# One of a body's four weight loads issued behind the key and query writes instead of in front of them

## The reference

```python
q, k, v = layernorm(x) @ Wq + bq, ctx @ Wk + bk, ctx @ Wv + bv      # split into 16 heads
attn = softmax(where(mask, -1e15, q @ k.T / 4))
x = x + tanh(g_xattn) * ((attn @ v) @ Wo + bo)
y = layernorm(x)
w = top 3 of softmax(tanh(mean(y) @ W1 + b1) @ W2 + b2), scaled to sum 1
x = x + tanh(g_ffn) * (y + sum over e of w[e] * (gelu(y @ Wa[e]) @ Wb[e]))
```

## Time and profile before

| | us |
|---|---|
| median of 3 runs | 319.05 (318.33 to 320.27) |
| the profiled execution | 319.47 |
| span of its profile | 317.7 |
| first phase, to the first matmul of the feed-forward | about 192.4 |
| TensorE busy | 293.0 (92%) |
| granted TensorE clock, mean | 0.973 |

### The profile page before, as it was taken

How to read it: one execution, slowest core, us unless ns; L and a number is a source line. 1 busy time by engine, 2 the same in 40 slices (tenths; PEclk the granted TensorE clock), 3 DMA queues, 4 the chain that set the end, 5 groups by cost and what they waited for, 6 DMA issues and landing times.

```text
span 317.7 us, 10417 instructions
## 1 busy us (share of the span) xinstructions
PE 293.0 (92%) x3968; PEld 242.0 (76%) x3968; DVE 227.3 (72%) x648; ACT 223.8 (70%) x439; POOL 136.4 (43%) x191
## 2 busy tenths in 40 slices
PE   7876997997999999999899876999999999999996
PEld 6642675775777767777567556999999999999996
DVE  5359685675787986879667675886886878767773
ACT  3541775884888878788677874867676976766773
POOL 4493385867769867688489541000100000000000
PEclk9995799998999999999999997999999999999999
DMA  6468978875878897777964550110211001010101
GB/s 167 122 181 222 261 181 230 218 208 150 219 188 237 209 268 203 197 192 204 226 161 135 174 155 2 32 31 2 62 32 32 23 25 47 2 46 5 31 2 31
DMA packets 38417, 40.59 MB, mean 128 GB/s; under 512 B 9800, under 2 KB 34032, under 8 KB 38368
## 3 DMA queue, kind: packets, MB, share of 16 engines
q1 hardware_dynamic: 37216, 38.48, 44.7%
q0 software_dynamic: 608, 0.92, 1.1%
q10 hardware_dynamic: 544, 0.52, 0.5%
HBM read 33.09 MB, written 6.74 MB: 125 GB/s over the span
## 4 chain that ended last, share of the span: by engine, by line
PE 61%; DMA 17%; DVE 7%; SPq 5%; ACT 4%; issue 4%; POOL 1%; DVEq 0%; ACTq 0%
PE bank L1370 17%; PE bank L1397 16%; DMA k_scr<-wb 8%; PE bank L1199 5%; DMA qbd<-q_scr 4%; PE bank L1181 4%; PE bank L1147 4%; PE bank L1159 3%; PE bank L1163 3%; SPq L352 2%; PE bank L1190 2%; DMA stage<-in_L_ffn_Wa 2%; DVE bank L866 2%; DMA ctx_s<-in_ctx 1%; PE bank L1208 1%
## 5 line engine op out<-in xcount | busy, mean ns | idle before, releaser
L866 DVE CUSTOM_DVE_ANT_0 bank<-bank,maskb 112x375 f32<-112x375 f32 x128 | 67.8, 569 | 27.1 <-PE bank L1147 26.6
L1370 PE MATMUL bank<-ctxT,wqkvo 128*128 128x112 f16 x960 | 60.9, 215 | 5.3 <-DVE qbd L999 5.3
L1370 PEld LDWEIGHTS bank<-ctxT,wqkvo 128*128 128x128 f16 x960 | 57.8, 99 | 6.0 <-issue 6.0
L1397 PE MATMUL bank<-stage,pT 128*128 128x112 f16 x1104 | 58.1, 213 | 0.0
L597 ACT ACTIVATE pT<-bank 125x448 f32<-125x448 f32 x96 | 50.2, 538 | 9.8 <-PE bank L1163 9.4
L1397 PEld LDWEIGHTS bank<-stage,pT 128*128 128x128 f16 x1104 | 55.8, 98 | 0.3
L503 POOL TENSOR_SCALAR stage<-stage 128x512 f32<-128x512 f32 x64 | 39.2, 629 | 37.0 <-DMA stage<-in_L_ffn_Wa 25.4
L1147 PE MATMUL bank<-kst,qbd 128*112 128x375 f16 x128 | 36.0, 350 | 10.2 <-DMA qbd<-q_scr 6.0
L1370 PE MATMUL bank<-ctxT,qbd 128*128 128x112 f16 x192 | 41.3, 215 | 0.0
L1159 PE MATMUL bank<-rq,maskb 115*128 115x448 bf16 (+1 forms) x96 | 35.9, 374 | 1.8 <-ACT pT L597 1.1
L812 ACT ACTIVATE pT<-wb 128x1024 f16 x23 | 24.3, 1056 | 15.9 <-PE bank L1397 13.8
(11 more groups left out here) (143 smaller groups left out, 495.0 us busy)
## 6 DMA issues: line engine op xcount, KB each, us to landing
stage<-in_L_ffn_Wa SPq DMA_DIRECT2D x16, 512.0 KB, 4.8
stage<-in_L_ffn_Wb SPq DMA_DIRECT2D x16, 512.0 KB, 4.1
kst<-k_scr SPq DMA_DIRECT2D x64, 93.8 KB, 3.8
k_scr<-wb SPq DMA_DIRECT2D x16, 187.5 KB
ctx_s<-in_ctx SPq DMA_DIRECT2D x8, 336.0 KB
qbd<-q_scr SPq DMA_DIRECT2D x24, 56.0 KB, 3.3
xa<-in_x SPq DMA_DIRECT2D x8, 112.0 KB, 4.7
q_scr<-wb SPq DMA_DIRECT2D x16, 56.0 KB, 3.4
```

Of the source, the lines that this page charges most:

```text
L866: v.tensor_tensor_reduce(out=bank[0:SQ, e, 0:SK], in0=bank[0:SQ, e, 0:SK], in1=maskb[0:SQ, b % 2, 0:SK], scale=-1.0, scalar=FLOOR, op0=ALU ...
L1370: ins = T.matmul(o, first(ws, t, f), x2b[:, b % 2, (xs * DT + t) * SQ:(xs * DT + t + 1) * SQ], start=(t == 0 and xs == 0 and ws == 0), sto ...
L1397: ins = T.matmul(o, second(u, ws * (2 * CHUNK) + f * D + t * 128), hT[:, u % 2, hs * FT * SQ + f * SQ:hs * FT * SQ + (f + 1) * SQ], start= ...
```

## The change

In SP's program, inside the loop over the bodies, `load_parts(b, 1)` moves from in front of `write_k(m, 0)` to behind `write_q(m)`. The number, the size and the waits of the transfers stay as they are.

```diff
@@ -448,10 +448,10 @@
                     load_ctx(m + 1)
                     load_x(m + 1)
                 load_mask(m)
-                load_parts(b, 1)
                 write_k(m, 0)
                 write_k(m, 1)
                 write_q(m)
+                load_parts(b, 1)
                 move_max(n, 0)
                 load_parts(b, 2)
                 if b == B - 1:
```

## The result

The changed kernel took 339.43 us (334.15 to 341.63, 4 runs), the kernel before 318.69 beside it. Two of the four executions were slow ones, with a granted clock of 0.955; the ratio of 1.054, 95% interval 1.041 to 1.067, is that of the other two, 336.1 on average, to 318.9. The sign was forecast, the size was not: 327.5, range 320.0 to 334.0. The profiled execution took 338.06, against 319.47 for that of before: 18.6 us more.

A forecast was written before the change was run, and what follows sets the result against it. It took TensorE as more than half the chain, nearly full in the first phase, with ScalarE lacking room towards GpSimd. Body terms summing to 8.0 us on the profiled 319.47 gave 327.5 us, range 320.0 to 334.0.

The forecast's parts named there:

- GpSimd's piece, 4.12 + 1.98: GpSimd, body 4: scaling through slot 2's low parts 4.12 us, then slot 3's scaling and the norm 1.98.
- "faster" rival: Key and query round trip: quicker key writes save 3.0 us, fewer query waits 3.0; 313.5 us, chance 0.08.
- the first term, the landing: Moved `Wb` load: lands 4.1 us after issue at the end of the query writes, at 133.6 in body 4.
- the forecast of 8.0: Sum over bodies 0 to 5: 0 + 0.8 + 2.6 + 1.3 + 2.3 + 1.0 us added.
- The prediction's own upper bound: Landing of 5.8 us in bodies 1 to 4: 1.7 us more in each, 334.3 us in all.
- The 3.2: Landing of the 512 KB load by the skill page's fit, 2.0 us plus bytes at 436 GB/s; not adopted.
- about 3: With the skill page's shorter landing, the whole sum would be about 3 us smaller.
- less the 1.58 us that ScalarE sat: Body 1: norm 2.6 us late, less ScalarE's idle 1.58 before 76.11 and 0.2, gives +0.8.
- 1.3: Body 3: L638 2.6 us late, less ScalarE's idle 1.10 and 0.24, gives +1.3 us.
- The high parts of slot 3: ScalarE's L707: first part scaled by 134.2, L707 began at 134.45, so no cost; load 1 us later loses the cover.
- Body 5: No norm in slot 3; next load held for low parts until 157.4; between nothing and 3.0 us, taken as +1.0.
- "slower still" rival: SP's 3.0 us hold in slot 3 passes on, delaying next body's loads and reads; 4.5 us more, 332; chance 0.14.

The follow-up runs named there:

- run 13: Changed kernel with the moved load of bodies 0 to 5 put behind the Wa load of SP's slot 2 too: 350.25 us, 1.106.
- run 9: Changed kernel with the moved load issued from ScalarE's transfer queue, behind its copy of the maxima in slot 2: 340.41 us, 1.059.
- run 11: Changed kernel with the Wa load of SP's slot 2 (bodies 0 to 5) put behind the key and query read-backs: 345.85 us, 1.092.
- run 12: Changed kernel with the Wa load of SP's slot 2 (bodies 0 to 5) in place but bringing only its first part: 339.06 us, 1.070.
- Run 10: Changed kernel with the moved load of bodies 0 to 5 bringing only its first part, 256 KB: 325.74 us, 1.023.
- run 1: Changed kernel with GpSimd's norm of b+3 moved from slot 3 to the head of slot 2, ahead of the late scaling: 336.36 us, 1.060.
- run 3: Kernel before, with the load moved in body 5 alone: 323.53 us, 1.018.
- run 5: Changed kernel with GpSimd's low parts of slot 2 made ahead of the scaling that waits for the moved load: 340.51 us, 1.080.
- run 6: Changed kernel with GpSimd's low parts of slot 2 and the norm of b+3 both ahead of the late scaling: 334.19 us (325.99 to 343.98).
- run 8: Kernel before, with the load issued behind both key writes and in front of the query writes: 329.37 us (324.98 to 329.98).

## Why the prediction was right or wrong

**Right in sign and road.** The load is late, GpSimd stands behind it, and ScalarE behind GpSimd. The length of GpSimd's piece, 4.12 + 1.98, came out as 6.1; the second phase did not change; the gains of the "faster" rival did not appear, and TensorE's waits for queries rose. L638 waited 8.9 us more in total, where some 9 were named, but that agreement is luck: this wait is 3.04 in a body whatever the lateness (run 13), and the rest went to L707, which the prediction had covered. Bodies 2 to 4 were to be 1 to 3 us longer each and were 0.8, 2.6 and 3.9 longer.

**Wrong in the first term, the landing.** The step "From issue to landing the 16 `Wb` loads took 3.9 to 5.8 us, 4.1 in the middle. So it lands at 133.6" took a middle from other places. Of those 16 loads ten were in other slots; the six in this very place (bodies 0 to 5) had 4.0 to 5.2, and behind the writes it became 5.7. At one microsecond per body, 1.6 us too little in six bodies is 9.6 of the 10.6 that the forecast of 8.0 is short of the 18.6. The prediction's own upper bound put the longer landing into four bodies only. The 3.2 that it worked out, as an estimate, from the fit in the Trainium skill's page "DMA: Bandwidth & Descriptors", section "Anatomy of one DMA", was further off still: in the kernel before no `Wb` load landed in under 3.9 us, in the changed one none in under 3.8. And 0.9 less in bodies 1 to 5 takes more off the sum, some 4 us, than the "about 3" of the text.

**What stretches the landing** stays open. It is not the queue (run 9), and not the `Wa` load behind (runs 11, 12). The key and query writes ahead may hold part of the transfer engines while the load lands. But the figures do not order by them: with no write ahead it landed in 4.6, behind one in 5.7, behind two in 5.3, behind four in 5.7. And in body 4 of the changed kernel, in the microsecond behind the query writes, 138 to 139, the engines were only 0.46 busy at 97 GB/s, while from 141 to 144, with the key and query reads under way, they were full at 319 to 334 GB/s. No run took the writes or the reads away.

**Wrong in how lateness was turned into time.** The step "less the 1.58 us that ScalarE sat" and its like took each body's late norm and subtracted what ScalarE idled. Body 3 by itself measured 3.4, not 1.3. The lateness is not one stall in a body: the end of the query writes starts the load, the load's norm starts L638, and L638's successors (exponentials, output copy, keys, queries) end in the next query writes, 11.4 us on. That is a closed chain, and its period is 11.4 + 6.1 + the lateness: 23.2 for 5.7, 23.1 measured in body 4, where the bodies before took 20 to 21.5. Run 10 shortened the one link and the time followed 1 for 1; run 13 lengthened it and 349 was forecast where 350.25 came. The norm is not the only way round: in run 1, with L638 only 2.95 us behind the scaling, the next query writes ended 13.2 to 15.7 us behind it, and the time stayed.

**Wrong in three terms taken as nothing or little.** The high parts of slot 3 were "covered: the first part is scaled by 133.6 + 0.6 = 134.2 and L707 began at 134.45". The cover was 0.25 us and the text said what its loss would do; with the true landing L707 waited 10.1 us. "Body 5" with its "+1.0" cost 5.8 alone (run 3). Its load landed 2.2 later than by the middle that I used; the next load, held for the low parts, went out at 160.3 and not at 157.4. And TensorE's clock is in no term: its longer waits were followed by stretches at 0.50, and its matmuls of the first phase took 5.6 us longer. How much of that lies on the path no run shows, as none held the clock.

**The "slower still" rival** had SP held before the next load as its place, and that hold is there, 30.5 us in total. But it is not where the rest lies: run 5 takes the hold away and gains nothing in the median, while TensorE's wait for queries and SP's for the maxima grow. The roads (norm, held load, high parts, query reads) seem near enough to each other that relieving one shows the next (runs 1, 5, 6). Every run that clearly changed the time changed the lateness, by the place of the load, its size or the number of bodies, except run 11, where most of the difference stands beside a lower clock.

## What to carry to other kernels

When a transfer is moved behind others, look for what starts it and follow its consumers until they come back to that starter. If they do, the body is a loop, its lateness counts in full in every body beyond the slack (here between 2.4 and 3.6 us), and idle time elsewhere must not be subtracted. Take the duration of a transfer from rows in which the same neighbours are in flight, not from the middle of all of its kind, and where three waits are nearly equal do not expect a repair of one to show. Where TensorE waits longer, look at its granted clock behind the wait before you put the whole time down to the wait.

## What the runs showed of the hardware

A 512 KB load that GpSimd waited for in other slots of the kernel before landed in 4.0 to 4.5 us. Behind the scratch writes of 0.49 MB it took 4.3 to 7.1, mostly over 5.2, from either of two queues (the change and runs 1, 5, 6, 9, 11, 12); half of it there landed in 3.6. Putting it on ScalarE's queue cost 0.37 us of ScalarE's issue and gained nothing.

TensorE's granted clock fell from 1.00 to 0.50 behind waits of 3.44 and 2.00 us in the changed kernel (before 179.75 and 199.24) and behind one of 2.63 us in run 8, where it stayed low for about 10 us; behind a wait of 2.6 us in body 4 of run 11 it did not fall. Of the four executions of the changed kernel the shortest, 334.15 us, had the highest mean clock, 0.974, and the longest, 341.63, one of 0.955.
